# Transposing rows and context outside TensorE in a transformer block: blocks turned through DRAM, 32x32 transposes on VectorE, one spreading transfer

## The reference

```python
def _attention(xq, xkv, wq, wk, wv, wo, bo):
    q = (xq @ wq).reshape(B, S, 16, 64)
    k = (xkv @ wk).reshape(B, T, 16, 64)
    v = (xkv @ wv).reshape(B, T, 16, 64)
    attn = softmax(einsum('bihd,bjhd->bhij', q, k) * 64 ** -0.5)
    return einsum('bhij,bjhd->bihd', attn, v).reshape(B, S, 1024) @ wo + bo
h = _layernorm(x, ln1_g, ln1_b)
x = _attention(h, h, sa_wq, sa_wk, sa_wv, sa_wo, sa_bo) + x
h = _layernorm(x, ln2_g, ln2_b)
x = _attention(h, cond_emb, ca_wq, ca_wk, ca_wv, ca_wo, ca_bo) + x
h = _layernorm(x, ln3_g, ln3_b)
p = h @ ff_w1 + ff_b1
h = p[..., :1024] * gelu(p[..., 1024:]) @ ff_w2 + ff_b2
return h + x
```

## Time and profile before

| what | value |
|---|---|
| median of 3 runs | 1752.76 us (1751.39 to 1754.06) |
| the profiled execution's own time | 1751.38 us |
| its span in the profile | 1749.6 us |
| PE busy | 1723.8 us (99%) |
| DVE, ACT, POOL busy | 1440.9, 1183.9, 1059.3 us |
| DMA engines busy, mean of 16 | 54.5% of the span for the kernel's queue |
| TensorE clock granted | 0.999 of full speed |

### The profile page before, as it was taken

The page is one execution under the profiler, slowest core; times in us unless marked ns, Lnnn a source line. Parts: engine busy times, 40 slices in busy tenths (PEclk is TensorE's granted clock), DMA queues, the critical chain, the costliest instruction groups (busy, mean ns, idle before and its releaser), DMA issues.

```text
span 1749.6 us, 43081 instructions
## 1 busy us (share of the span) xinstructions
PE 1723.8 (99%) x13824; PEld 1687.3 (96%) x13824; DVE 1440.9 (82%) x3137; ACT 1183.9 (68%) x3262; POOL 1059.3 (61%) x1791
## 2 busy tenths in 40 slices
PE   6999999999999999999999999999999999999998
PEld 6999999999999999999999999999999998888887
DVE  6888888888888888888888888888888897666664
ACT  5777777777777777777778777788777775221121
POOL 4787777766666666787777777666666664100100
PEclk9999999999999999999999999999999999999999
DMA  7776666666565555666667776666666661001000
GB/s 197 193 168 171 162 163 163 161 170 156 139 145 141 141 145 143 150 164 163 177 176 174 178 176 164 166 166 153 155 155 152 153 148 41 25 25 49 13 13 25
DMA packets 226496, 241.31 MB, mean 138 GB/s; under 512 B 68448, under 2 KB 190688, under 8 KB 226272
## 3 DMA queue, kind: packets, MB, share of 16 engines
q1 hardware_dynamic: 226272, 238.55, 54.5%
HBM read 58.08 MB, written 12.58 MB: 40 GB/s over the span
## 4 chain that ended last, share of the span: by engine, by line
PE 97%; DVE 1%; POOL 1%; issue 1%; ACT 0%; DMA 0%; DVEq 0%; POOLq 0%; ACTq 0%
PE QKB L294 20%; PE PVB L354 14%; PE PTB L340 13%; PE WOP L327 10%; PE VB L313 10%; PE S L261 7%; PE S L262 7%; PE S L758 5%; PE PTB L758 5%; PE VB L771 3%; PE QKB L771 3%; PE VB L236 1%; PE VB L249 0%; ACT PT L410 0%; PE PVB L737 0%
## 5 line engine op out<-in xcount | busy, mean ns | idle before, releaser
L410 ACT ACTIVATE PT<-S,NM 128x256 f32<-128x256 f32 x1024 | 471.8, 474 | 152.4 <-DVE NM L477 150.9
L465 DVE TENSOR_TENSOR PL<-PTB,PH 128x512 fp32r<-128x512 f32 x512 | 351.0, 686 | 152.9 <-ACT PH L429 149.2
L429 ACT ACTIVATE PH<-PTB 128x1024 fp32r<-128x1024 f32 x256 | 263.1, 1028 | 134.2 <-PE PTB L340 131.0
L656 POOL TENSOR_TENSOR ON<-ON,RB 128x256 f32<-128x256 f32 x256 | 188.4, 736 | 269.4 <-DVE ON L488 266.7
L477 DVE TENSOR_REDUCE NM<-S 128x2 f32<-128x512 f32 x512 | 326.3, 679 | 0.0
L340 PE MATMUL PTB<-IDN,PT 128*128 128x128 f32 x2048 | 266.1, 273 | 2.3 <-DVE PL L465 2.3
L261 PE MATMUL S<-RX 128*128 128x256 f32 x1024 | 256.9, 283 | 2.1 <-ACT PT L410 2.1
L262 PE MATMUL S<-RX 128*128 128x256 f32 x1024 | 256.8, 283 | 0.0
L340 PEld LDWEIGHTS PTB<-IDN,PT 128*128 128x128 f32 x2048 | 229.7, 140 | 3.2 <-DVE PL L465 3.2
L327 PE MATMUL WOP<-WO,OT 128*128 128x256 f32 x1536 | 226.5, 283 | 0.9 <-POOL OT L661 0.8
L294 PE MATMUL QKB<-HT,WA 128*128 128x256 f32 x1536 | 211.8, 288 | 6.6 <-POOL HT L561 3.6
(11 more groups left out here) (113 smaller groups left out, 3133.6 us busy)
## 6 DMA issues: line engine op xcount, KB each, us to landing
RX<-QKS SPq DMA_DIRECT2D x512, 192.0 KB, 2.9
RX<-QKS SPq DMA_DIRECT2D x512, 128.0 KB, 2.8
RB<-denominators SPq DMA_DIRECT2D x512, 64.0 KB, 2.6
out_dram<-XR SPq DMA_DIRECT2D x32, 256.0 KB, 3.0
XR<-in_x_dram SPq DMA_DIRECT2D x16, 256.0 KB, 3.1
denominators<-RDT SPq DMA_DIRECT2D x256, 16.0 KB
XR<-out_dram SPq DMA_DIRECT2D x16, 256.0 KB, 3.0
XN<-in_ctx_dram SPq DMA_DIRECT2D x16, 192.0 KB, 2.8
```

Source lines behind the costliest of these rows:

```text
L410: last = e.activation(PT[:, c % 2, j * S:(j + 1) * S], S1[:, i, qt * S:(qt + 1) * S], ACT.Exp, bias=NM[:, j:j + 1], accum_out=DEN[:, c % 2 ...
L429: e.activation(PH[:, s % 2, :], PTB[:, :, :].rearrange("p i n -> p (i n)"), ACT.Copy) \
L465: e.tensor_tensor(PL[:, cols], PTB[:, i, :], PH[:, s % 2, cols].bitcast(F32), ALU.subtract).then_inc(a.dve_pl, 1)
```

## The change

Rows of x are no longer transposed on PE. `dve_normalize` writes them to `HF` with their blocks of 32 columns regrouped. SP stores them to DRAM (`store_rows`, one transfer, at pair 0) and loads them back with the blocks of 32 rows moved to the partitions where they belong (`load_rows`, four transfers, at pair 1). DVE then turns every 32x32 block in one instruction (`dve_turn_rows`, at pair 2), and ACT and POOL do gain, bias and splitting one pair later than before. The context is loaded by blocks of 32 columns, in eight transfers of 256 pieces of 128 bytes (six at pair 5, two at pair 6), turned by DVE at the end of its slot of pair 6 (`dve_turn_ctx`), and split by POOL from `XN`; ACT's copy of it is gone. Statistics and normalization move up (pairs 4, 5 and 7 of the sequence before). The feed-forward chunks get the same treatment with 2 stores, 8 loads and 4 half-size turns each. `spread_den` becomes one transfer of 128 partitions.

```diff
-        def pe_h(e, sl, n, k, bank=VB):
+        def pe_first_rows(e, k, bank):
...
-        def pe_ctx(e, sl, n, k):
...
-            if prepares:
-                n = seq + 1
-                if pair in (0, 1) and n >= B or pair in (2, 3):
-                    sl.wait(e, a.dve_vf, c + 1)
-                if pair in (0, 1) and n >= B:
-                    pe_ctx(e, sl, n, pair)
-                if pair in (2, 3):
-                    pe_h(e, sl, n, pair - 2)
...
+        def dve_turn_rows(e, n):
+
+            e.wait_ge(d_hl, 64 * n)
+            e.transpose(HF[:, :].rearrange("p (g b j) -> p g b j", g=2 * TT, b=4),
+                        XN[:, :].rearrange("p (b g i) -> p g b i", b=4, g=2 * TT)).then_inc(a.dve_th, 1)
+
+        def dve_turn_ctx(e, sl, m):
+
+            e.wait_ge(d_cx, 128 * (m + 1))
+            sl.wait(e, a.pl_ct, 2 * m)
+            e.transpose(XN[:, :], HF[:, :]).then_inc(a.dve_tc, 1)
...
+            if prepares and pair == 2:
+                dve_turn_rows(e, seq + 1)
+            if pair == 6 and sl.has(PAIRS * (seq + 2)) and seq + 2 >= B:
+                dve_turn_ctx(e, sl, seq + 2 - B)
+            if pair == 7 and sl.has(PAIRS * (seq + 2)):
+                sl.wait(e, a.pl_ht, 2 * (seq + 2))
+                dve_normalize(e, sl, a, seq + 2, (HF[:, :],))
...
-            if c >= 0 and c % PAIRS == 5 and sl.has(c + PAIRS):
-                if chunk == 0:
-                    e.wait_ge(a.dve_xo, 2 * B)
-                    e.wait_ge(a.dve_ad, ATT)
-                pe_ffn_h(e, sl, chunk + 1)
...
-            def load_ctx(n):
-                e.wait_ge(a.pe_h, 2 * (n + B))
-                src = ctxt[sequence(n + B), :, :].rearrange("(t p) d -> p t d", p=P)
-                e.dma_start(CX[:, :, 0:DC], src).then_inc(d_cx, 16)
-                e.dma_start(CX[:, :, DC:S], src[:, :, P:DC]).then_inc(d_cx, 16)
+            def load_ctx(n, *pieces):
+                e.wait_ge(a.pl_ht, 2 * (n + B))
+                src = ctxt[sequence(n + B), :, :]
+                for piece in pieces:
+                    k, part = divmod(piece, 4)
+                    col = k * P + (part - k * 2 * (part // 2)) * 32
+                    e.dma_start(HF[part * 32:(part + 1) * 32, k * S:(k + 1) * S].rearrange("j (g i) -> j g i", i=32),
+                                src[:, col:col + 32].rearrange("(g j) i -> j g i", j=32)).then_inc(d_cx, 16)
...
+            def load_turned(dst, src, done):
+
+                for q in range(4):
+                    e.dma_start(dst[q * 32:(q + 1) * 32, :].rearrange("j (b f) -> j b f", b=4),
+                                src[:, q * P:(q + 1) * P].rearrange("(b j) f -> j b f", b=4)).then_inc(done, 16)
...
-                for i in range(2):
-                    e.dma_start(RB[OWN[i], s % 2, :],
-                                DS[s % 4, TT * i:TT * (i + 1), :].rearrange("t p -> (t p)").partition_broadcast(P // 2)) \
-                        .then_inc(d_rb[s % 2], 16)
+                den = DS[s % 4, 0:2 * TT, :]
+                e.dma_start(RB[:, s % 2, :],
+                            bass.AP(tensor=den.tensor, offset=den.offset, ap=[[S, 2], [0, P // 2], [1, S]])) \
+                    .then_inc(d_rb[s % 2], 32)
...
                 if pair == 5 and B - 2 <= seq < 2 * B - 2:
-                    load_ctx(seq - B + 2)
+                    load_ctx(seq - B + 2, *range(6))
+                if pair == 6 and B - 2 <= seq < 2 * B - 2:
+                    load_ctx(seq - B + 2, 6, 7)
+                if pair == 0 and 0 <= seq < 2 * B - 1:
+                    store_rows(seq + 1)
+                if pair == 1 and 0 <= seq < 2 * B - 1:
+                    load_rows(seq + 1)
```

More of the change, by code:

```diff
@@ L224, in block_kernel @@
         attentions = (Attention(0, WA), Attention(1, WB))
[L227 to L234 removed]
+        def pe_first_rows(e, k, bank):
+            e.wait_ge(a.dve_xn, 1)
             for t in range(TT):
@@ L302, in pe_slot @@
                 sl.wait(e, a.dve_vf, v)
-                if prepares and pair in (0, 1) and seq + 1 >= B:
-                    sl.wait(e, a.act_cf, 2 * (seq + 1 - B) + pair + 1)
-                if prepares and pair in (2, 3):
-                    sl.wait(e, a.act_hf, 2 * (seq + 1) + pair - 1)
                 if v == 0:
@@ L662, in pool_slot @@
                                 ALU.subtract).then_inc(a.pl_o, 1)
-            if prepares and pair == 0:
-                pool_rstd(e, sl, a, seq + 1)
+            if pair == 5 and sl.has(PAIRS * (seq + 2)):
+                pool_rstd(e, sl, a, seq + 2)
         NCK = B // 2
@@ L708, in block_kernel @@
         OB = (QKB, VB)
-        def halves(chunk):
-            if chunk == 0:
-                return XN[:, :], HF[:, :]
-            return HF[:, :], RB[:, :, :].rearrange("p r s -> p (r s)")
-        def rows(chunk):
-            return (STG[:, 0:CW], STG[:, CW:2 * CW]) if chunk == 0 else halves(chunk)
-        def transposes(chunk):
-            return (QKB, QKB) if chunk == 0 else (PVB, WOP)
+        ROWS = (XN[:, :], HF[:, :])
+        TURNED = (STG[:, 0:CW], STG[:, CW:2 * CW])
         def w1(k, part, col):
@@ L729, in w2 @@
             return WA[:, 4 + f // 4, part, (f % 4) * D:(f % 4 + 1) * D]
-        def pe_ffn_h(e, sl, chunk, *ks):
-            sl.wait(e, fs.dve_xn, chunk + 1)
-            for k in ks or range(KD):
-                sl.wait(e, fs.act_hf, KD * chunk + (k if ks else 0))
-                for t in range(2 * TT):
-                    col = t % TT * D + k * P
-                    last = e.transpose(transposes(chunk)[k][:, t * P:(t + 1) * P],
-                                       halves(chunk)[t // TT][:, col:col + P], IDN[:, :])
-                last.then_inc(fs.pe_ht, 1)
         def pe_ffn(e, sl):
@@ L775, in pe_ffn, with act_ffn_h @@
                 last.then_inc(fs.pe_f2, 1)
-            if c >= 0 and c % PAIRS == 5 and sl.has(c + PAIRS):
-                if chunk == 0:
-                    e.wait_ge(a.dve_xo, 2 * B)
-                    e.wait_ge(a.dve_ad, ATT)
-                pe_ffn_h(e, sl, chunk + 1)
-        def act_ffn_h(e, sl, chunk, *ks):
-            for k in ks or range(KD):
-                sl.wait(e, fs.pe_ht, KD * chunk + k + 1 if ks else KD * (chunk + 1))
-                e.activation(rows(chunk)[k], transposes(chunk)[k][:, :], ACT.Identity,
-                             bias=LNG[:, 2, 1, k:k + 1], scale=LNG[:, 2, 0, k:k + 1]).then_inc(fs.act_hf, 1)
+        def act_ffn_h(e, chunk, k):
+            e.wait_ge(fs.dve_th, 2 * (chunk + 1))
+            e.activation(ROWS[k], ROWS[k], ACT.Identity, bias=LNG[:, 2, 1, k:k + 1],
+                         scale=LNG[:, 2, 0, k:k + 1]).then_inc(fs.act_hf, 1)
         def act_ffn(e, sl):
@@ new lines, in load_rows, with store_ffn_rows @@
+            def load_rows(n):
+                e.wait_ge(d_hs, 16 * n)
+                if n >= B:
+                    e.wait_ge(a.pl_ct, 2 * (n - B + 1))
+                elif n > 1:
+                    e.wait_ge(a.dve_th, n - 1)
+                else:
+                    e.wait_ge(a.pe_h, 2)
+                load_turned(XN[:, :], HS[0, :, :], d_hl)
+            def store_ffn_rows(chunk):
+                e.wait_ge(fs.dve_xn, chunk + 1)
+                if chunk:
+                    e.wait_ge(d_fl, 128 * chunk)
+                for h in range(2):
+                    e.dma_start(HS[1 + h, :, :], ROWS[h]).then_inc(d_fs, 16)
@@ L966, in _, with load_ffn_rows @@
+            def load_ffn_rows(chunk):
+                e.wait_ge(d_fs, 32 * (chunk + 1))
+                if chunk:
+                    e.wait_ge(fs.dve_th, 2 * chunk)
+                else:
+                    e.wait_ge(s_pw, 2 * QTR * NCH)
+                for h in range(2):
+                    load_turned(TURNED[h], HS[1 + h, :, :], d_fl)
             half = DA // 2
```

180 lines of the change are left out of this document (91 added, 89 removed).

## The result

| | before | after |
|---|---|---|
| median of the timed runs | 1752.8 us | 2020.6 us (2015.1 to 2024.3) |
| ratio, 95% interval | | 1.1526 [1.1493, 1.1559] |
| span of the profiled execution | 1749.6 us | 2022.4 us |
| mean granted TensorE clock | 0.999 | 0.962 |

The change costs 268 us. The forecast was 1793 us in a range of 1725 to 1855: slower was right, the size was not.

What follows compares the result with a forecast made beforehand. PE, busy 99% of the span, was taken to bound the kernel. Transposes -28, late context and two-engine spread +66, feed-forward +2 gave +40 us on the profiled 1751.4; with 1.4 for the median, 1793 us, range 1725 to 1855.

Steps and rivals of the forecast that it cites:

- Term 1: Attention and feed-forward: PE loses 252 transposes at 0.11 us each, all on the chain, -28 us.
- Term 2: DVE's block turns, 0.6 us each, are covered by its idle time and cost nothing; 28 us if that cover goes.
- Term 4: Attention slots: the merged spread runs on two DMA engines, loaded 5.26 us per slot; together with the late context +66 us.
- I take 1.84: Ring copies on the spread's two engines: assumed to take 1.84 us per slot, against 2.77 before the change.
- Rival C: Ring copies stay at 2.77 us per slot on the spread's two engines: about 2005 us; beyond 1855, chance 0.08.
- Term 3: Cross attention: the context lands late, DVE waits 4.0 us and PE idles about 2.4 in 16 sequences, +38 us.
- Term 5: Feed-forward: DVE may wait for stores and loads before a chunk's first turn, 2 us in all.
- Rival A: The merged spread keeps its 16 DMA engines and costs nothing: +12 us, 1765 us, chance 0.17.
- rival B: Reserves cover the late context and the two engines never decide, so PE's gain stands: 1727 us, chance 0.13.

## Why the prediction was wrong

Right were the direction, the engine count and the first term. Wrong by size were terms 3 and 4, together +66 where the runs show 240 (53 and 187), and the sum had no term for another 31.

**Term 1, -28.** Borne out by the doubled transposes, +27.5; of the 56 in the feed-forward stage, taken away alone, 4.6 of 6.2 us came back.

**Term 2, nothing for the turns.** They take 0.71 us, I had 0.6. Without the pieces the context's turn is worth 6 us (1751.1 to 1745.0), so "covered by idle time" holds but for 0.4 us each.

**Term 4, the spread on two engines.** This is the step that failed. The two engines were right. The step was "I take 1.84" for the ring copies, and under it the idea that a load below the slot's length is hidden. The merged spread costs 187 us on the changed kernel, where the sum had 28 for it (66 less term 3's 38). Where the sum had self sequences fitting at 5.45 us, the slots were 6.2 to 6.4. Rival C's 2.77 for the ring copies gave 2005 us for the whole kernel and I gave it 0.08 (its sum covers 248 of the 256 slots; the other 8 add 6 us). It comes close in time, but that is partly luck, for its reason is only part of it: swapping save and spread gave 72 us back at the same load, and left such slots at 5.7 to 6.0 us, 0.3 to 0.5 above the sum. If the load alone sets them, the ring copies take 2.1 to 2.3 us, between both values (an estimate from 5.45 and 1.84). I had written that SP waits for the save before each spread and given it no price. It is a loop: spread, save behind it on the same two engines, landing 5.8 us after the issue, next spread, with SP's ring copies held up in it and ACT held up by those.

**Term 3, the late context, +38.** The wait of DVE was well put (4.0; 4.49 in the place shown, 5.3 as a mean of 85.1 over 16). The cost was 53 us. The reserve that ran out first was not one of the two counted but that of `PL`, directly behind the turn. Even so the idle time of PE came to 31 us, under the 38; what the sum lacked were the 22 us of busy time at the lower clock that followed. In the changed kernel itself the wait is 7.3 us, and 6.2 (99.6 over 16) with save and spread swapped: the merged spread holds up the pieces too. The rows' own loads, called in time, nearly were: DVE waits 11.4 us for them, in 12 places.

**Not in the sum at all: the queue's own time.** The six issues that the context adds were used only to date the last piece. They also stand ahead of the ring copies of two slots, for 31 us (1780.9 to 1750.2). "SP enters pair 6 1.9 us late" was in my text; who waits for the ring copies it delays (ACT at L385) wasn't followed.

**Term 5, +2.** About right: from the last save to the end it is 288.1 us before and 283.7 with the turn in pair 7, so 4.4 of the 6.2 us that 56 transposes are worth come through. The FFN alone gains 4.6.

**Together**: 187 + 53 + 31 - 28 = 243 of the 268, each cost as it fell away in this order (the merged spread costs 204 on the kernel before). The remaining 25 are the difference of the run with a plain context (1750.2) to 1725. By the times between saves, held against before less its transposes, they lie in the first two sequences (about 6), the cross sequences with staged weights (8) and the last seven attention slots (6, where the FFN's first turns stand); no run isolates these, and some 5 are in no particular place. Rival A failed at the merge, which it had as free, and by the same other costs; rival B asked for a context less than 1.9 us late and slots under 5.42 us, and neither came.

## What to carry to other kernels

Price an added DMA first by its issue on the queue, and follow who stands behind it there to the first compute engine that waits: six more transfers per sequence, each 0.5 to 0.6 us of the queue, cost 31 us, and their bytes next to nothing. Look at the outermost dimension of a merged transfer's pattern, since the merge can put its whole load on few engines. A load that "fits the slot" still costs its latency once per trip of a loop through it (save, land, spread), so look for the loop before adding loads. And where removing one named wait after another changes nothing, leave work out instead: one run without the pieces told more than four mended waits.

## What was not expected of the hardware

- A transfer whose DRAM pattern begins with 2 ran with a DMA share of 0.11 to 0.16, and the 16 KB save behind it landed after 5.8 us. With 4 at the front the same bytes cost nothing (1.0011). The completion writes give the engines away: 2, 4 and 8 per slot in place of 32.
- After PE had been idle for 2.8 of 4 us, the granted clock stood at 0.50 (the 1.2 GHz level) from 1254 to 1257, PE being busy again, then at 0.90 and 1.00. PE's two gaps there were 1.94 and 1.08 us. Fourteen such places, 78 us at 0.50, make most of what the run's mean of 0.975 lacks, and 22 us of its time.
- DVE's 32x32 turns of a 128x512 fp32 tile take 0.71 us, hardly more than an elementwise pass of that size (0.65 to 0.69).
- A DMA issued by GpSimd takes 599 ns of that engine, as much as an issue on SP's queue.
